# Key feature map and head mask moved from VectorE to ScalarE and GpSimd, with the fourth group's residual one unit later

## What is computed

```python
k, v = jnp.split(kv @ Wkv.T, 2, axis=-1)
k = jnp.where(k > 0, k + 1.0, jnp.exp(k))           # the feature map
kv_summary = jnp.einsum('bhsd,bhse->bhde', k, v)    # per head, 16 heads of 16 features
k_sum = k.sum(axis=-2)
```

## Time and profile before

| | |
|---|---|
| median of three runs | 520.44 us (517.2, 520.44, 521.5) |
| the profiled execution | 518.78 us, of it 517.0 us from the first to the last instruction |
| TensorE | 451.1 us busy, 87% of the span |
| VectorE | 359.8 us, 70% |
| ScalarE | 249.2 us, 48% |
| GpSimd | 153.2 us, 30% |
| granted clock of TensorE, mean | 0.965 of full |

### The profile page before, as it was taken

How to read it: one execution, slowest core, us unless ns; L and a number is a source line. 1 busy time by engine, 2 the same in 40 slices (tenths; PEclk the granted TensorE clock), 3 DMA queues, 4 the chain that set the end, 5 groups by cost and what they waited for, 6 DMA issues and landing times. The chain is left out here.

```text
span 517.0 us, 7223 instructions
## 1 busy us (share of the span) xinstructions
PE 451.1 (87%) x2134; PEld 355.4 (69%) x2142; DVE 359.8 (70%) x1034; ACT 249.2 (48%) x454; POOL 153.2 (30%) x156
## 2 busy tenths in 40 slices
PE   1617899988999989999999999998998799899991
PEld 1305688656678767788778787787776588788860
DVE  6896779896389798565987967888778354621173
ACT  3618574753575363337044317270751444955540
POOL 3955342220002021100000000050525014477781
PEclk9966999998999998999999999999999899999996
DMA  8510312000200003950000000132423223346394
GB/s 305 186 31 30 103 31 82 1 0 21 83 1 0 2 0 99 280 123 0 2 0 1 1 1 1 32 118 68 126 76 102 92 74 92 114 147 201 90 387 146
DMA packets 32965, 42.00 MB, mean 81 GB/s; under 512 B 3483, under 2 KB 26781, under 8 KB 32928
## 3 DMA queue, kind: packets, MB, share of 16 engines
q1 hardware_dynamic: 28224, 32.28, 21.2%
q0 software_dynamic: 3744, 8.42, 4.4%
q10 hardware_dynamic: 960, 0.86, 0.5%
HBM read 24.97 MB, written 18.39 MB: 84 GB/s over the span
## 5 line engine op out<-in xcount | busy, mean ns | idle before, releaser
L658 PE MATMUL acc<-w_down,act_s 128*128 128x256 f32 x384 | 90.5, 381 | 0.9 <-DVE act_s L1384 0.9
L658 PEld LDWEIGHTS acc<-w_down,act_s 128*128 128x128 f32 x384 | 73.1, 191 | 12.5 <-DVE act_s L1384 1.3
L634 PE MATMUL ring<-xt_h,up_l 128*128 128x512 f32 x160 | 70.5, 440 | 4.8 <-DVE xt_l L1354 3.3
L635 PE MATMUL ring<-xt_l,up_h 128*128 128x512 f32 x160 | 63.9, 399 | 0.0
L636 PE MATMUL ring<-xt_h,up_h 128*128 128x512 f32 x160 | 63.8, 399 | 0.0
L1599 POOL TENSOR_TENSOR rstd<-var_eps,minus_half 128x4 f32<-128x4 f32 x14 | 15.0, 1068 | 163.8 <-DVE var_eps L1184 163.8
L1096 ACT ACTIVATE act_s<-ring 128x512 f32<-128x512 f32 x48 | 28.7, 598 | 65.8 <-PE ring L636 65.6
L629 PE MATMUL ring<-small,xn 128*128 128x128 f32 x160 | 23.7, 298 | 27.4 <-ACT xn L996 14.4
L697 PE MATMUL ring<-up_e,act_s 128*128 x184 | 45.3, 389 | 2.3 <-issue 2.0
L1635 POOL DMA_INDIRECT x_rows<-main_a,slots x32 | 31.1, 970 | 43.7 <-ACT main_a L1117 34.8
L1388 DVE TENSOR_TENSOR act_s<-ring,act_s 128x512 f32<-128x512 f32 x32 | 22.1, 690 | 28.1 <-PE ring L636 18.5
(11 more groups left out here) (275 smaller groups left out, 984.3 us busy)
## 6 DMA issues: line engine op xcount, KB each, us to landing
main_b<-x_rows SPq DMA_DIRECT2D x22, 257.0 KB, 3.0
x_rows<-v_t SPq DMA_DIRECT2D x1, 3983.5 KB, 18.4
up_l<-y_rows SPq DMA_DIRECT2D x5, 512.0 KB, 6.2
stage<-in_w_mlp SPq DMA_DIRECT2D x8, 256.0 KB, 2.7
up_e<-in_w_moe SPq DMA_DIRECT2D x8, 256.0 KB, 2.7
x_rows<-v_t SPq DMA_DIRECT2D x1, 1927.5 KB, 24.7
x_nat<-in_x SPq DMA_DIRECT2D x7, 256.0 KB, 7.6
out_x<-x_nat SPq DMA_DIRECT2D x6, 256.0 KB, 5.8
```

What stands on the lines that cost most here:

```text
L634: pe.matmul(out, wl, xh, start=first, stop=False, skip_group_check=True)
L635: pe.matmul(out, wh, xl, start=False, stop=False, skip_group_check=True)
L658: last = pe.matmul(acc[t // 2][:, t % 2, :], act_s[n % RING][:, tok], w_down[:, u, :], start=u == 0 and t % 2 == 0, stop=final, skip_group ...
```

## The change

ScalarE now makes all of the feature map but one addition. It writes relu(-k) into `k_e`, relu(k) into `k_r`, copies the values and frees the bank; then it makes exp(-relu(-k)) = min(exp(k), 1) in place. GpSimd adds `k_r` to it and raises `k_ready`. The bank V is copied to `kv_sum` unmasked by ScalarE (`copy_sums`), and GpSimd applies the mask later, four sequences at a time, in new steps `mask g 0 1 2 3`. ScalarE's and GpSimd's parts are a step of their own, `feat g t`, which the list sets right behind `kv g t`. TensorE waits for all masks once, ahead of the first attention step of `attn` 4. The residual and moments of WKV group 3 stand in unit 12 of main 1 and no longer in unit 11.

The table of steps, two of its lines:

```diff
-        11: "wkv_out 3 6 7, x_stats 3 0, kv 3 2 3, mlp_in 2 0",
-        12: "kv 3 4, clear 0 0, mlp_in 2 1",
+        11: "kv 3 2 3, mlp_in 2 0",
+        12: "wkv_out 3 6 7, x_stats 3 0, kv 3 4, clear 0 0, mlp_in 2 1",
```

`mask 0` is put behind `route 0 4 5 6` in unit 5 of main 0, `mask 1` in unit 2 and `mask 2` in unit 6 of main 1, `mask 3` at the head of the steps after unit 12 of main 1. The engines' parts:

```diff
+for n in range(len(SCHED) - 1, -1, -1):
+    if SCHED[n][0] == "kv" and ("feat", *SCHED[n][1:]) not in SCHED:
+        SCHED.insert(n + 1, ("feat", *SCHED[n][1:]))
...
+                        once("sums", sums_masked, NSEQ)
...
+            def copy_sums(g, t):
+
+                if t >= 0:
+                    key = (("kv", g), "V", t)
+                    bank = full(act, key)
+                    act.activation(kv_sum[:, wkv_seqs(g)[t], :], bank[:, 0:C * KVW], ACT.Copy).then_inc(free_sem(key), 1)
...
-                elif kind == "kv" and part < GT:
+                elif kind == "feat" and part < GT:
...
-                    act.activation(k_e[n % 2][:, :], bank[:, 0:D], ACT.Exp)
+                    act.activation(k_e[n % 2][:, :], bank[:, 0:D], ACT.Relu, scale=-1.0)
                     act.activation(k_r[n % 2][:, :], bank[:, 0:D], ACT.Relu)
                     act.activation(v_x[n % 2][:, :, 0:P], bank[:, D:].rearrange("p (c m) -> p c m", c=C),
                                    ACT.Copy).then_inc(free_sem((step, "K", t)), 1)
+                    freed(act, (step, "K", t))
+                    act.activation(k_e[n % 2][:, :], k_e[n % 2][:, :], ACT.Exp, scale=-1.0).then_inc(k_exp, 1)
+                    copy_sums(g, t - 1)
+                elif kind == "feat":
+                    copy_sums(g, part - 1)
...
-                        dve.scalar_tensor_tensor(k_e[n % 2][:, :], k_e[n % 2][:, :], 1.0, k_r[n % 2][:, :], ALU.min,
-                                                 ALU.add).then_inc(k_ready, 1)
...
-                        free((step, "V", t - 1), dve.tensor_tensor(
-                            kv_sum[:, seqs[t - 1], :].rearrange("p (c m) -> p c m", c=C),
-                            bank[:, 0:C * KVW].rearrange("p (c m) -> p c m", c=C),
-                            head_mask.unsqueeze(1).broadcast_to([P, C, KVW]), ALU.mult))
...
+                elif kind == "feat" and part < GT:
+                    n = g * GT + part
+                    pool.wait_ge(k_exp, n + 1)
+                    pool.tensor_tensor(k_e[n % 2][:, :], k_e[n % 2][:, :], k_r[n % 2][:, :], ALU.add).then_inc(k_ready, 1)
+                elif kind == "mask":
+                    freed(pool, (("kv", g), "V", part))
+                    pool.wait_ge(later_loaded, 16)
+                    sums = kv_sum[:, wkv_seqs(g)[part], :].rearrange("p (c m) -> p c m", c=C)
+                    pool.tensor_tensor(sums, sums, head_mask.unsqueeze(1).broadcast_to([P, C, KVW]),
+                                       ALU.mult).then_inc(sums_masked, 1)
```

More of the change, by code:

```diff
@@ L457, in build @@
         y_ready = sem("y_ready")
+        k_exp = sem("k_exp")
         k_ready = sem("k_ready")
+        sums_masked = sem("sums_masked")
         diff_ready = sem("diff_ready")
@@ L1012, in _ @@
                     act.activation(own, own, ACT.Copy, scale=own_weight[:, c:c + 1]).then_inc(own_scaled, 1)
-                elif kind == "kv" and part < GT:
+                elif kind == "feat" and part < GT:
                     t = part
                     n = g * GT + t
+                    step = ("kv", g)
                     bank = full(act, (step, "K", t))
```

## The result

The change makes the kernel slower: 530.48 us against 519.53 us for the kernel before in the same comparison, a ratio of 1.0241 (95% interval 1.0202 to 1.0281). A second comparison gave 529.41 against 516.85, 1.0238 (1.0204 to 1.0272). Each comparison has its own runs of the kernel before, whose median lies between 516.17 and 519.53, so kernels are compared by their ratios to it. The forecast was 524.5 with a range of 518.5 to 530.0 and "within 1%" as the likeliest case; both were wrong, the range by half a microsecond.

The account below looks back on a forecast made before the run. TensorE, busy in 87% of the span, was taken as the bound, VectorE counting only where TensorE waits for it. The terms summed to +4.3 us on the profiled 518.78, 523.1; on the median 524.5, range 518.5 to 530.

Parts of the forecast that it names:

- c: Group 0's masks on GpSimd, beside route 0: they hold up VectorE, loss 0.9 us (between 0 and 2.7).
- a: Start: an addition stands ahead of y's second half, yet the first half is read earlier; gain 0.4 us.
- b: `kv 0 2` to `kv 0 4`: Silu later behind load, Exp and copy; loss 1.9 us, plus 1.0 for the clock.
- d: Main 0 to main 1: main 1's first matmul later, loss 0.7 us, plus 1.7 for a lower clock.
- e: kv 2: Silu 1.5 to 2.2 us late in four units, but its result is used later; taken as nothing.
- f: End of main 1: y a unit later shortens TensorE's wait; gain 1.5 us (0.9 to 2.2).
- GpSimd holds up VectorE throughout: Rival, chance 0.16: additions at `kv 1` and `kv 3` and masks of groups 0 and 3 hold up VectorE; 530 us.
- A change of table costs more than the load: Rival, chance 0.08: a load delays by more than its 1.28 us, 1.4 dearer at b and at d; 527.3 us.
- The lateness is hidden: Rival, chance 0.14: ScalarE's load runs early after all, so b and c cost nothing and d gains; 516.6 us.

Follow-up runs that it names:

- both kernels with the old map: The changed kernel with the feature map as before, ratio 1.0056 to before; the same with mask 0 a unit earlier and mask 3 in main 2, 0.9991.
- both remedies: The changed kernel with an Exp of one column ahead of each wait for bank K, mask 0 a unit earlier, mask 3 in main 2: 519.42 us against 516.85, 1.0039.

## Why the prediction was wrong, step by step

The sum was +4.3; the trace has +9.8, 5.5 more, and c alone is 3.7 of it. By the sum's letters, with what was measured in the table's first column:

| step | forecast | measured |
|---|---|---|
| a, start | -0.4 | +1.7 |
| b, `kv 0 2` to `0 4` | +1.9, clock +1.0 | +2.3, clock 0 |
| c, masks beside route 0 | +0.9 | +4.6 |
| d, main 0 to main 1 | +0.7, clock +1.7 | +0.1, clock +2.8 and +1.3 |
| e, kv 2 | 0 | +0.2 |
| f, end of main 1 | -1.5 | 0.0 |
| not in the sum, the rest | 0 | -1.9 |

**c is the step that failed most.** "VectorE gets an instruction in where one mask ends and the next begins, so I put its loss at 1.2 of the 3 us" undersized a mechanism that was right: VectorE does get one in between each two masks, but each of them waits for the end of the mask that runs, and it lost 2.2. And the upper bound, "the masks in full", was no bound. It left out that a late VectorE meets the next GpSimd instruction, a split that had started 0.05 us behind VectorE's one-hot products; that cost 1.4. The lower clock behind the wait of 3.44 us adds 1.05, which the term for c did not have at all.

**a had the wrong sign.** The addition was priced at 0.73, the duration of an instruction that ran alone. At the start the change brings VectorE's scans forward, and they met just these additions (timelines, before and after):

```profile
29.05 2.95 DVE L1235 TENSOR_TENSOR_SCAN q_pad<-decay,xt_f_pad 128x516 f32<-128x516 f32 x2
...
26.38 3.42 DVE L1255 TENSOR_TENSOR_SCAN q_pad<-decay,xt_f_pad 128x516 f32<-128x516 f32 x2
...
27.06 1.65 POOL L1624 TENSOR_TENSOR k_e<-k_e,k_r 128x256 f32<-128x256 f32 x1
28.67 2.19 POOL L1617 TENSOR_TENSOR main_a<-main_a,main_b 128x512 f32<-128x512 f32 x1
```

With the masks on VectorE a mask waits for bank V ahead of the scans and so keeps them out of the way:

```profile
29.46 3.43 DVE L1244 TENSOR_TENSOR_SCAN q_pad<-decay,xt_f_pad 128x516 f32<-128x516 f32 x2
...
26.89 0.72 POOL L1622 TENSOR_TENSOR k_e<-k_e,k_r 128x256 f32<-128x256 f32 x1
27.57 1.28 POOL L1615 TENSOR_TENSOR main_a<-main_a,main_b 128x512 f32<-128x512 f32 x1
```

1.65 and 2.19 against 0.72 and 1.28: 1.84 us, and TensorE's transposes of y start at 32.26 against 30.25. The start as a whole gains less from it, 0.77 of 1.67, because in the kernel with masks on VectorE the scans end the wait: they start 0.41 later than before, behind the mask, and take 0.48 longer beside the next addition, together the 0.90 that it loses. In both kernels with the old map, which has no additions on GpSimd, nothing is lost at the start (-0.11 and -0.14). So the work taken from VectorE did not shorten the start; it moved VectorE's reading onto GpSimd's, and y, which the path runs through, is GpSimd's.

**b was right in mechanism and size.** Silu comes 3.3 us after the last reading ends and TensorE waits 2.50, as said. Of the 2.3, 2.0 stand at that wait. The clock stayed at 1.00 behind it, so the 1.0 for it was wrong.

**d was right in kind.** The wait is 3.56 (forecast 3.8) and the clock fell to the lower level (0.50). The 0.7 of the first part did not show (0.1). The clock's price was taken from one fall of before; the falls here cost 1.3 to 2.8.

**f was right about the wait that it removed and wrong about what comes next.** Alone the move gains 4.7 and gives back 1.8, 2.9 in all, better than forecast. In the changed kernel 2.1 of the first go to an addition that stands behind y on GpSimd (206.64, wait of 1.95; 1.1 was forecast for it), and masks 3 hold up the normalisations, 4.45 instead of 2.67 us (timelines, before and after):

```profile
207.63 2.67 DVE L1199 TENSOR_SCALAR xn<-x_nat,mean_rstd,rstd 128x256 f32<-128x256 f32 x8
...
219.12 4.45 DVE L1219 TENSOR_SCALAR xn<-x_nat,mean_rstd,rstd 128x256 f32<-128x256 f32 x8
...
219.33 3.11 POOL L1629 TENSOR_TENSOR kv_sum<-kv_sum,later 128x272 f32<-128x272 f32 x4
```

It is the move that brings the two together. Without it the same masks, at the same place in the list, were done at 217.4, the eight normalisations behind them took 2.67 again, and the end of main 1 lost nothing (-0.02).

**The rivals.** "GpSimd holds up VectorE throughout", at 530, was the one that came true in time, with a chance of 0.16. Its argument against itself, that much of VectorE's work does not lengthen, holds (reductions keep 0.42, MAX8 1.10); but the masks were placed beside the part of route 0 that does. Its sum is not what happened, and that it hit the time is in part luck: of its additions at `kv 1` nothing is seen on balance (0.1 on the way to main 1), while the loss at the start (1.7) and the clock's behind route 0 (1.05) were not in it. "A change of table costs more than the load" is out: the load taken off the path gave back its own 1.28 in both waits. "The lateness is hidden" is out too; yet its premise, a load that runs early, can be made with one column of Exp, and is worth 3.5 us in the changed kernel by the spans (526.8 and 523.3), 1% by the ratios (1.0238 and 1.0133).

Shown by taking the cause away: the masks' places (4.6 at route 0, about 1.1 to 1.8 at the end of main 1) and the load's place (1.28 at `kv 0 2`, 1.28 in the wait ahead of main 1, 1.7 in unit 10), and that the start's loss goes with the additions. Shown by one pair of traces only: that it is the scans that they meet there. Open: the move's worth in the changed kernel (0.4 us by place, 3 by the ratios), and what decides whether the clock falls and how long it stays low.

## What to carry over

An instruction given to GpSimd is priced not by its own length but by what VectorE runs beside it: look up in the timeline whether that reads two operands from SBUF or is a normalisation or a CAST (all three were held up here), and then shift VectorE by what it loses and look which GpSimd instruction it meets next. A load of a function table that was hidden by a wait stays hidden only while an instruction that needs the table stands ahead of the wait. And take a bundle of edits apart: here the one that moved a step a unit later, which needs nothing of the rest, gains 0.6% alone and was buried under a loss of 3.0%, the ratio of the kernel without it.

## What was not expected of the hardware

- A CAST of VectorE with one input, 32 columns wide, took 1.94 us instead of 0.18 while GpSimd ran memsets, while products with two inputs beside the same memsets kept their 0.18 and 0.41.
- VectorE's normalisation, a TENSOR_SCALAR, is held up by GpSimd as well: four took 3.23 us beside masks and 1.90 with less GpSimd work beside them.
- The collision works both ways: beside scans GpSimd's addition took 1.65 instead of 0.72 us, and beside that addition and a product of GpSimd the two scans took 3.42 instead of 2.95 us.
- The clock does not answer to the length of a wait alone: behind 2.28 us of waiting it fell in the kernel with the early load (1.59 us lost) and not in the one with both remedies (0.02), behind 2.50 us at `kv 0 2` not at all, and one wait of 3.56 us cost 2.81 in one trace and 1.30 in another of the same kernel.
